# Early loads, short edge tables, an edge softmax in tiles and a slot search inside the experts' loop, in a four-layer graph and expert kernel on one core

## The reference, cut to what matters

```python
x = x + gcn(layernorm(x), src, dst, ...)          # 3 layers: batch norm, sum over edges, @ W, relu
x = x + expert_choice(layernorm(x), ...)          # 32 experts, each takes its best 312 tokens
x = x + edge_attention(layernorm(x), [src, dst], edge_attr_8, ...)
x = x + top2(layernorm(x), ...)                   # 8 small experts, 2 per token

# expert choice                                   # edge attention (rows = src, cols = dst)
G, idx = top_k(softmax(x @ Wr).T, 312)            logits = (q[rows] * scale . k[cols]) + att_bias
up   = silu(x[idx] @ W_up[e // 4] + b_up)         p   = exp(logits - segment_max(logits, rows)[rows])
out  = G * (up @ W_down[e] + b_down)              att = p / segment_sum(p, rows)[rows]
y    = zeros.at[idx].add(out)                     out = segment_sum(att * v[cols], rows) @ Wo + bo
```

## Time and profile before

| | |
|---|---|
| median of 3 runs (lowest, highest) | 3903.74 us (3902.39, 3907.45) |
| the profiled execution | 3906.87 us, its span 3905.1 us |
| busy, share of the span | PE 83%, PEld 70%, DVE 63%, ACT 36%, POOL 32% |
| TensorE's granted clock, mean | 0.886 of full |
| bytes moved by DMA | 449.60 MB, 115 GB/s in the mean |

### The profile page before, as it was taken

One profiled execution on the slowest core, in us unless ns is written; L12 is line 12 of the kernel. 1 busy time (PEld: TensorE's weight loads), 2 busy tenths in 40 slices (PEclk: granted clock), 3 DMA queues, 4 the chain that ended last, 5 costly groups with the idle time before them and its releaser, 6 DMA issues. The chain is left out here.

```text
span 3905.1 us, 61914 instructions
## 1 busy us (share of the span) xinstructions
PE 3254.1 (83%) x18334; PEld 2750.4 (70%) x18335; DVE 2462.7 (63%) x5844; ACT 1388.0 (36%) x2580; POOL 1235.2 (32%) x1606
## 2 busy tenths in 40 slices
PE   6845889997775309999999999999679992969999
PEld 1213667776774209999999999999668881856766
DVE  7855877644766764545455444454278877957776
ACT  4633655421112314445444444444211111114443
POOL 4752532222551012323222322323123320025552
PEclk9977999997555559999999999999889995989999
DMA  4313323335994034544444444444322111146663
GB/s 157 99 24 105 106 94 122 100 124 167 305 306 135 0 76 113 133 116 136 126 111 137 102 133 143 99 137 113 66 64 59 54 43 42 67 122 149 161 155 104
DMA packets 250361, 449.60 MB, mean 115 GB/s; under 512 B 65632, under 2 KB 71073, under 8 KB 249591
## 3 DMA queue, kind: packets, MB, share of 16 engines
q1 hardware_dynamic: 176425, 280.66, 22.0%
q0 software_dynamic: 62368, 145.38, 17.1%
q10 hardware_dynamic: 11318, 20.54, 1.4%
HBM read 319.38 MB, written 126.83 MB: 114 GB/s over the span
## 5 line engine op out<-in xcount | busy, mean ns | idle before, releaser
L1460 PE MATMUL experts_psU<-experts_x_hi,experts_up_hi 128*128 128x312 f32 (+1 forms) x1408 | 443.3, 315 | 22.9 <-issue 16.5
L1489 PE MATMUL experts_psY<-experts_hid_hi,experts_dn_hi 128*128 128x312 f32 (+1 forms) x1408 | 439.0, 312 | 0.0
L1461 PE MATMUL experts_psU<-experts_x_lo,experts_up_hi 128*128 128x312 f32 (+1 forms) x1408 | 436.8, 310 | 0.0
L1462 PE MATMUL experts_psU<-experts_x_hi,experts_up_lo 128*128 128x312 f32 (+1 forms) x1408 | 435.6, 309 | 0.0
L1490 PE MATMUL experts_psY<-experts_hid_lo,experts_dn_hi 128*128 128x312 f32 (+1 forms) x1408 | 431.3, 306 | 0.0
L1491 PE MATMUL experts_psY<-experts_hid_hi,experts_dn_lo 128*128 128x312 f32 (+1 forms) x1408 | 429.7, 305 | 0.0
L1419 POOL DMA_INDIRECT experts_xg<-xn,experts_token_i x96 | 123.4, 1285 | 663.0 <-DVE experts_token_i L1586 643.5
L1625 DVE TENSOR_TENSOR experts_hid_lo<-experts_hid,experts_hid_hi 128x312 fp32r<-128x312 f32 (+1 forms) x352 | 161.2, 480 | 252.2 <-ACT experts_hid L1552 252.2
L1550 ACT ACTIVATE experts_hid_hi<-experts_psU,experts_bup 128x312 fp32r<-128x312 f32 (+1 forms) x352 | 183.6, 522 | 322.1 <-PE experts_psU L1462 320.3
L1460 PEld LDWEIGHTS experts_psU<-experts_x_hi,experts_up_hi 128*128 128x128 f32 (+1 forms) x1408 | 265.2, 188 | 24.4 <-issue 22.0
L1617 DVE TENSOR_TENSOR experts_dn_lo<-experts_dn_raw,experts_dn_hi 128x1536 fp32r<-128x1536 f32 (+1 forms) x128 | 208.0, 1625 | 98.6 <-ACT experts_dn_hi L1528 98.4
(11 more groups left out here) (412 smaller groups left out, 8158.7 us busy)
## 6 DMA issues: line engine op xcount, KB each, us to landing
experts_dn_raw<-in_L_ffn_W_down SPq DMA_DIRECT2D x96, 768.0 KB, 4.6
conv<-gcn_diff SPq DMA_DIRECT2D x120, 256.0 KB, 2.9
experts_up_raw<-in_L_ffn_W_up SPq DMA_DIRECT2D x32, 682.5 KB, 8.4
index_xt<-in_x SPq DMA_DIRECT2D x78, 256.0 KB, 2.8
route_xt<-in_x SPq DMA_DIRECT2D x78, 256.0 KB, 4.9
x<-route_xt SPq DMA_DIRECT2D x78, 256.0 KB, 4.3
xn<-route_xn ACTq DMA_DIRECT2D x78, 256.0 KB, 5.0
two_xt<-x SPq DMA_DIRECT2D x78, 256.0 KB, 2.8
```

The source lines that it names most:

```text
L1460: pe.matmul(acc, up_hi[:, c, cols], x_hi[:, c, :], start=(c == 0), stop=False)
L1461: pe.matmul(acc, up_hi[:, c, cols], x_lo[:, c, :], start=False, stop=False)
L1462: mm = pe.matmul(acc, up_lo[:, c, cols], x_hi[:, c, :], start=False, stop=(c == C - 1))
L1489: pe.matmul(acc, dn_hi[0:w, m, cols], hid_hi[0:w, m, :], start=(m == 0), stop=False)
```

## The change

It touches eight places:

1. `gcnt`: the neighbours are compared on 40 partitions (`link` is [40, 128]) against a loaded column `nextkey`; `key` comes in four pieces with a semaphore each; the sums of `adj` gather in one PSUM tile of ten rows, split once. SP also loads `edgeS` and its shifted copy `prevS` here (5,120 pieces of 48 bytes each), and DVE keeps `joinsS` (does an edge have the source of the edge ahead of it).
2. `gcn0`: the four first gathers and the moment chain are done in `gcnt`.
3. `choose`: SP loads the first up weights into a lasting tile `stage`; the last running sum is written as 16-bit integers (`upto_slot`); POOL makes `slot` and `expert`.
4. `slots` is gone. The loop's `stage` searches the slots of one expert in seven DVE instructions.
5. `experts`: one `y` buffer, so that `weigh` waits for the scatter of the expert before it; behind the loop SP loads Wq and Wk into `stage`.
6. `score`: only Wv is loaded there; its parts are made behind the first tile's.
7. `weigh`: 128 partitions hold 16 edge tiles by 8 heads, three such groups of 128 edges along the row. A pass scans each piece, sends the pieces' ends through PE into one row of 40, scans that, hands the carries back through PE, and scans again.
8. `two`: the first four tiles of `x` are issued ahead of the weights.

The core of the diff:

```diff
@@ gcn_tables
+            sp.dma_start(g.edgeS[:, :, :], g.recS[1:EP + 1, :].rearrange("(t p) c -> p t c", p=P)).then_inc(g.edges, 16)
+            sp.dma_start(prevS[:, :, :], g.recS[0:EP, :].rearrange("(t p) c -> p t c", p=P)).then_inc(g.edges, 16)
+            sp.wait_ge(cleared, 1)
+            sp.dma_start(nextkey[0:ET - 1, :], ...).then_inc(following, 16)
             sp.wait_ge(copied, 1)
...
-            sp.dma_start(key[:, 0:ET, :].rearrange("p t l -> p (t l)"), g.rowsD[0, :].partition_broadcast(P))\
-                .then_inc(rows, 16)
+            for k in range(ET // CH):
+                sp.dma_start(key[:, k * CH:(k + 1) * CH, :].rearrange("p t l -> p (t l)"),
+                             g.rowsD[0, k * CH * P:(k + 1) * CH * P].partition_broadcast(P)).then_inc(key_in[k], 16)
...
+        @block.gpsimd
+        def _(pool):
+            pool.wait_ge(loaded, 32)
+            for s in range(R):
...
+                pool.indirect_dma_start(g.xt0[:, s, :], None, x, bass.IndirectOffsetOnAxis(ap=idx[:, s, :], axis=0))\
+                    .then_inc(g.gathered0[s], 16)
...
-            v.tensor_tensor(link[:, :].rearrange("o (t l) -> o t l", l=P), key[0:1, 0:ET, :],
-                            key[0:1, 1:ET + 1, 0:1].to_broadcast([1, ET, P]), ALU.is_equal).then_inc(linked, 1)
+            v.tensor_tensor(link[:, :], turned[:, :], nextkey[:, 0:1].to_broadcast([ET, P]), ALU.is_equal).then_inc(linked, 1)
@@ choose
+            for c in range(g.D // P):
+                sp.dma_start(g.stage[:, c, :], up_rows[c * P:(c + 1) * P, :]).then_inc(g.up_loaded[c], 16)
@@ experts, on VectorE
             def stage(e, j):
                 at_least(v, located, e, R, L)
-                v.tensor_copy(row_i[:, j, :], row[:, :, bass.ds(e, 1)].rearrange("p q o -> p (q o)")).then_inc(staged, 1)
+                upto = upto_slot[:, bass.ds(e, 1), :].to_broadcast([P, Q, TT])
+                seek.at(e)
+                seek(v.tensor_tensor(found[:, :, :], upto, slot[:, :].unsqueeze(2).to_broadcast([P, Q, TT]), ALU.is_le))
+                seek(v.tensor_reduce(tile_of[:, j, :], found[:, :, :], AX.X, ALU.add))
+                seek(v.tensor_tensor(found[:, :, :], found[:, :, :], upto, ALU.mult))
+                seek(v.tensor_reduce(filled[:, :], found[:, :, :], AX.X, ALU.max))
+                seek.go(v.tensor_tensor(rest[:, j, :], slot[:, :], filled[:, :], ALU.subtract))
+                seek(v.scalar_tensor_tensor(row[:, :], tile_of[:, j, :], float(X),
+                                            expert[:, bass.ds(e, 1)].to_broadcast([P, Q]), ALU.mult, ALU.add))
+                v.tensor_copy(row_i[:, j, :], row[:, :]).then_inc(staged, 1)
...
             def weigh(e, j):
-                pair_landed(v, scattered, e, j, Q, 2)
+                pair_landed(v, scattered, e, j, Q, 1)
@@ attention_weights, on VectorE
+            def forward(n, rows, data, low, op0, op1):
+                step(v.tensor_tensor_scan(flat(b), flat(rows), flat(data), low, op0, op1))
+                spread_of(b[:, :, P:P + 1])
+                step(v.memset(state[:, 0:1], low))
+                v.wait_ge(gathered, n + 2)
+                step(v.tensor_tensor_scan(state[:, 1:ET + 1], (barred if op0 == ALU.add else through)[:, 0:ET],
+                                          psK[0:H, 0:ET], low, op0, op1))
+                v.sem_inc(carried, 1)
+                take_carry(n, data[:, :, 0])
+                step(v.tensor_tensor_scan(flat(b), flat(rows), flat(data), low, op0, op1))
```

More of the change, by code:

```diff
@@ L607, in _ @@
             act.wait_ge(linked, 1)
-            act.activation(unlink[:, :], link[:, :].bitcast(F32), ACT.Identity, scale=-1.0, bias=g.ones[0:1, 0:1])\
+            act.activation(unlink[:, :], link[:, :].bitcast(F32), ACT.Identity, scale=-1.0, bias=g.ones[0:ET, 0:1])\
                 .then_inc(unlinked, 1)
-            for k in range(ET // G):
-                act.wait_ge(summed, k + 1)
-                act.copy(parts[:, 0, k * 512:(k + 1) * 512], psW[0:1, k % 2, :]).then_inc(high, 1)
+            act.wait_ge(summed, 1)
+            act.copy(parts[:, 0, :], psW[0:NG, :]).then_inc(high, 1)
         @block.vector
@@ L1054, in _, with choose @@
             step(v.memset(probs[:, NT:TT, :], -1.0))
-def choose(nc, g, probs, K, upto_tile, in_tile):
+def choose(nc, g, probs, K, upto_tile, in_tile, upto_slot, slot, expert, W_up):
     TT, X = probs.shape[1], probs.shape[2]
@@ L1380, in load @@
             def load(e, j):
[L1381 removed]
+                if j == 0 and not (isinstance(e, int) and e == 0):
                     for c in range(C):
@@ new lines, in _ @@
+            step(v.memset(state[:, :], 0.0))
+            v.wait_ge(joins_turned, 1)
+            for k in range(K):
+                r = rows_of(k)
+                step.go(v.tensor_copy(on[0:r, k, 1:P + 1], psG[0:r, k * P:(k + 1) * P]))
+            step.wait(step.n)
+            step.go(v.tensor_reduce(flags[:, :], on[:, :, 1:P + 1], AX.X, ALU.min))
+            step.go(v.tensor_scalar(flat(ahead), flat(on), -1.0, BIG, ALU.add, ALU.mult))
+            step.go(v.memset(astern[:, :, P:P + 1], 0.0))
@@ L2329, in program @@
             parts = -(-K // P)
-            tile_of, rest, row = (mid.sb(n, [P, parts, X]) for n in ("tile_of", "rest", "row"))
+            slot, expert = mid.sb("slot", [P, parts]), mid.sb("expert", [P, X])
+            upto_slot = mid.sb("upto_slot", [P, X, TT], I16)
             with Phase(nc, "probs") as sub:
```

454 lines of the change are left out of this document (301 added, 153 removed).

## The result

The changed kernel takes 3789.52 us (median of 4 runs, 3786.68 to 3790.94), the kernel before beside it 3905.16: a ratio of 0.9705, interval 0.969 to 0.9719. The forecast was 3783, in a range of 3763 to 3814. The profiled execution's span went from 3905.1 to 3786.9 us.

| stage | before | after | moved | forecast | same code |
|---|---|---|---|---|---|
| `index` | 273.3 | 275.1 | +1.8 | 0 | 273.7 to 275.7 |
| `gcnt` | 52.6 | 43.2 | -9.4 | -12 | 43.2 to 44.9 |
| `gcn0` | 224.4 | 215.2 | -9.1 | -8.7 | 215.1 to 215.4 |
| `route` | 304.2 | 300.2 | -4.1 | 0 | 294.5 to 302.0 |
| `slots` | 33.8 | gone | -33.8 | -33.8 | |

A forecast was written before the change was run, and what follows sets the result against it. The prediction took TensorE to bound the `experts` loop, and DVE or a transfer the other four stretches. Nine terms sum to -121.3 us, from 3906.9 to 3785.6, as a median 3783 us; range 3763 to 3814.

The forecast's parts named there:

- 1. `gcnt`: Stage `gcnt`: shorter DVE path and one split, less SP's delay by small pieces; -12 us, bounds -16 and -6.
- 2. `gcn0`: Head of `gcn0`: gathers and moment chain done before the barrier, first statistics at about +3.1; -8.7 us (-10 to -7).
- 4. Head of `experts`: Start of `experts`: bias loads already there, two searches added ahead of the first `find`; -5 us (-8 to 0).
- 5. Loop: Loop of `experts`: a 2.4 us search per expert fits in DVE's 4.44 us idle time; 0 us (0 to +10).
- 6. `score`: Head of `score`: `edgeS` already there, first statistics at about +9.3, 3 us charged for uncovered work; -16 us (-19 to -11).
- 7. `weigh`: Stage `weigh`: short scans with relays through matmuls replace four scans of 5,120 elements; -44 us (-48 to -36).
- 8. `two`: Head of `two`: wait for first rows goes, weights come later; 4.90 less 2.4, -2.5 us (-6 to 0).
- 9. The end: End of the kernel: one more barrier, since the outermost phase now owns semaphores; +0.7 us.
- early loads gain nothing: Rival for `gcnt`, `score`, `two`: the early-loading stage pays what the later one saves; 3813 us, chance 0.08.
- `weigh`'s small steps cost twice: Rival for `weigh`: the 22 us that are not long scans double, stage 51 us; 3805 us, chance 0.10.
- exposed search: Rival for the `experts` loop: TensorE waits 2.4 us per expert for the search; 3860 us, chance 0.05.
- lost clock: Rival for the `experts` loop: search stalls also drop TensorE's clock, 5.8 us per expert; 3969 us, chance 0.03.

The follow-up runs named there:

- edges_behind: Changed kernel with `edgeS` and `prevS` issued behind the loads of `key` in `gcnt`, ahead of the weights; 3794.28 us, ratio 0.9713.
- weights_in_index: Changed kernel with the fifteen layer weight loads issued by SyncE at the end of `index`, and `edgeS`, `prevS` behind `key`; 3782.61 us, ratio 0.9702.
- weights_act: Changed kernel with the fifteen weight loads of `gcnt` issued by ScalarE in place of SyncE; 3794.02 us, ratio 0.9721.
- search_four: Changed kernel with the four wide passes of the slot search standing four times in a row per expert; 3855.33 us, ratio 0.9875.
- lift_first: Changed kernel with VectorE and ScalarE lifting `yT` ahead of the last part of the next expert's down weights; 3783.12 us, ratio 0.9702.
- edges_in_score: Changed kernel with `edgeS` and `prevS` loaded at the head of `score` again, no longer in `gcnt`; 3790.53 us, ratio 0.9724.
- old_weigh: Changed kernel with the softmax stage `weigh` alone taken back to its earlier form; 3827.51 us, ratio 0.9812.
- two_weights_first: Changed kernel with the first four tiles of `x` in `two` issued behind the weights again; 3785.31 us, ratio 0.9708.
- search_eight: Changed kernel with the search's four wide passes standing eight times in a row per expert; 4047.23 us, ratio 1.0359.

## Why the prediction came out right, step by step

The sum said -121.3 us for the profiled execution, and 118.3 came. Nine terms, in the forecast's numbering:

1. `gcnt`, -12 forecast, -9.4 measured: mechanism right, size too large. Two charges were too small. The price of small pieces was read off one row, "`prev` costs SP's queue 2.90 us for 5,120 pieces", as if an issue paid for its own pieces. edges_behind shows that it pays for those ahead (`edgeS` 0.60 us, `prevS` 11.39), so `nextkey` with its 39 pieces took 4.11, which the sum had at nothing: `key` is issued 6.2 us later, not 5, and the weights' issue ends 34.2 us into the stage, not 32.6. And "SP reaches the last stores at about 314" allowed 2 us behind the weights' end; the stores of `link` and `unlink` stand there, and it took 3.2. So the last stores come 37.6 us into the stage, not 34.6, and the stage is 43.2 us, not 40.6. That SyncE's list ends the stage, and not `key`, is shown by edges_behind and weights_in_index; weights_act shows how far: with `key` another 13.5 us later it is `key`. The rule of the Trainium skill on a DMA's fixed and variable cost (page "DMA: Bandwidth & Descriptors", section "Anatomy of one DMA — SWDGE (gpsimd) path") is a fit to DMAs that GpSimd issues. Carried over to SyncE's two loads, as the prediction did, it gives an estimate of 1.1 us; SyncE was held 5.9 us by them and 4.11 by the next, so the trace goes against it for such pieces on that queue.
2. `gcn0`, -8.7 and -9.1: first statistics at +3.0, as said.
3. `slots`, -33.8 and -33.8.
4. Head of `experts`, -5 and -5.0.
5. Loop, 0 and 0 as a sum; the reason given for it was incomplete. The search is 1.95 us, not 2.4, and 2.49 us of idle time are left in the row that the forecast read, as foreseen. But that idle time is not the cover of every expert: each fourth has none, and what holds there is slack further down the chain of `dn_lo`, load and `yT`. search_four finds its end, and lift_first that `yT` held TensorE up slightly before the change already. One `y` buffer cost nothing that a row shows: no wait for a scatter stands in the lists of waits; a kernel with two buffers was not run.
6. `score`, -16 and -16.3, first statistics at +8.9 against +9.3. They come 19 us earlier and the stage is 16.3 shorter, so what isn't covered costs 2.6, charged at 3. edges_in_score gives 7 to 8 us of it to the early `edgeS`; the rest was not tried apart.
7. `weigh`, -44 and -44.4: a pass is 4.2 to 4.4 us (4.0 forecast), the setup 5.8 (6.7), so a part of the close hit is two errors that offset each other. old_weigh gives it back whole.
8. `two`, -2.5 forecast. The step that failed is "the weights, which come four DMAs later (2 us or more)": they come 5.0 us later, and VectorE's preparation, which waits for them, eats the whole gain (two_weights_first). The head gained 0.1 us; the other +2.3 us lie within what the stage varies by, and no cause is claimed.
9. The end, +0.7 and +0.4.

`route` moved by -4.1 and `index` by +1.8 with no change of theirs. By luck that offsets 2.3 of the 7.2 us by which terms 1 and 8 fell short.

Of the rivals: that early loads gain nothing is right in `two`, and half right for the two edge loads, which save 7 to 8 us in `score` and cost `gcnt` 3.7 to 5.4 (edges_in_score). That `weigh`'s small steps cost twice is wrong. The exposed search and the lost clock did not happen, but search_four and search_eight show that both mechanisms are real and come together: at four times the passes the loss is 2.0 us per expert, over a third of it clock. The wait, though, is for `yT` first, and for `x_lo` as well only at eight times.

## What to carry to other kernels

Where stages end at barriers, cost each from its own rows, and expect the sum to hold. An engine's idle time ahead of one instruction covers new work only in the turns of the loop that have it; look at the turn with the least, and follow what it delays through buffers and loads to the place where the slack ends. Here small-piece DMAs were paid by whatever stood behind them on the queue, and what helped was to put them last together with moving the bulk loads to a stage where the queue was idle; putting them last alone did not.

## What the runs showed of the hardware

How long a DMA's issue on SyncE took depended here more on what stood ahead of it than on its own pieces: a load of 39 pieces took 2.86, 4.11 and 14.66 us in three kernels, the longest with ScalarE's loads beside it, and of two of 5,120 pieces each (edges_behind) the first took 0.60 us and the one right behind it 11.39. A stall of TensorE of 4.22 us in search_four came with 6.8 us at the lower of its two clocks, in a loop that runs at 0.99 in the changed kernel. In the two runs with a longer search each microsecond of such waiting came with some 0.6 us lost by the clock.
